# Rows of a mixture of experts sent to their expert's region batch by batch, the weights awaited by expert, one clearing of semaphores a stage, and three operations of the last stage put elsewhere

## The reference

```python
x = x + L0_attn(norm(x), W)                 # windowed attention
x = x + L0_xattn(norm(x), ctx, mask, ...)   # cross attention to 77 context rows, 8 heads
x = x + L0_ffn(norm(x), router_w, W1, W2)   # 8 experts, each row uses one:
    #   top1 = argmax(h @ router_w + router_b); y = gelu(h @ W1[top1] + b1) @ W2[top1] + b2
x = x + L1_attn(norm(x), ...)               # two-part mixing with a scan over batches (wkv)
x = x + L1_xattn(norm(x), ctx, ...)         # top-32 attention, FiLM, state-space convolution, network
x = x + L1_ffn(norm(x), ...)                # product with signs, scale, bias, clip to +-100
```

## Time and profile before

| | us |
|---|---|
| median of 3 runs (lowest, highest) | 1900.02 (1899.65, 1901.29) |
| the profiled execution, its own time | 1900.81 |
| the span that its trace covers | 1899.1 |
| PE busy, share of the span | 1632.9, 86% |
| DVE busy | 1312.9, 69% |
| ACT busy | 866.0, 46% |
| POOL busy | 655.4, 35% |

### The profile page before, as it was taken

The page is one execution under the profiler, slowest core; times in us unless marked ns, Lnnn a source line. Parts: engine busy times, 40 slices in busy tenths (PEclk is TensorE's granted clock), DMA queues, the critical chain, the costliest instruction groups (busy, mean ns, idle before and its releaser), DMA issues.

```text
span 1899.1 us, 26400 instructions
## 1 busy us (share of the span) xinstructions
PE 1632.9 (86%) x7946; PEld 1260.9 (66%) x7946; DVE 1312.9 (69%) x4214; ACT 866.0 (46%) x1714; POOL 655.4 (35%) x1016
## 2 busy tenths in 40 slices
PE   5899999993199999993677999999999999998775
PEld 3677777772066766772555777777778777776544
DVE  2467777764047777542567899898889899987642
ACT  1344444441022111113555666777766667754331
POOL 1122222212500000004444566556556555543221
PEclk9899999996599999997788999999999999999876
DMA  8000000004844343435000000000000000000000
GB/s 261 19 1 1 1 1 1 1 1 154 327 129 137 100 118 98 129 114 191 6 6 6 7 12 12 7 12 12 12 6 12 12 6 7 7 6 7 0 6 11
DMA packets 81060, 92.91 MB, mean 49 GB/s; under 512 B 19142, under 2 KB 69527, under 8 KB 80667
## 3 DMA queue, kind: packets, MB, share of 16 engines
q1 hardware_dynamic: 72235, 77.73, 12.8%
q0 software_dynamic: 3072, 8.39, 1.3%
q10 hardware_dynamic: 5616, 5.11, 0.8%
HBM read 70.76 MB, written 20.45 MB: 48 GB/s over the span
## 4 chain that ended last, share of the span: by engine, by line
PE 26%; DVE 20%; issue 3%; ACT 2%; POOL 2%; DMA 0%; POOLq 0%; DVEq 0%; ACTq 0%
PE E_pK L2218 5%; PE E_pK L2177 3%; PE E_pS L2279 3%; DVE E_wk L1748 3%; DVE E_ex L1680 2%; PE E_pY L2326 2%; PE E_pY L2165 2%; PE E_pY L2297 2%; DVE E_m L1741 2%; PE E_pU L2288 1%; DVE E_st L1613 1%; PE E_pY L2177 1%; PE E_pT L2159 1%; PE E_pY L2228 1%; PE E_pU L2316 1%
## 5 line engine op out<-in xcount | busy, mean ns | idle before, releaser
L1226 ACT ACTIVATE F_uT<-F_puT 128x512 f32<-128x512 f32 x78 | 42.8, 595 | 287.5 <-PE F_puT L1287 256.5
L1277 PE MATMUL F_pu<-C_W,F_hT 128*128 x312 | 145.3, 610 | 1.2 <-issue 1.2
L1498 POOL TENSOR_SCALAR E_var<-E_mv 128x2 f32<-128x2 f32 x80 | 42.1, 527 | 292.9 <-DVE E_mv L1617 291.8
L1297 PE MATMUL F_py<-C_W,F_uT 128*128 x624 | 141.3, 380 | 0.5 <-ACT F_uT L1226 0.5
L2316 PE MATMUL E_pU<-E_xT,E_W 128*128 128x256 f32 x512 | 121.5, 393 | 7.2 <-ACT E_hid L2075 4.9
L1297 PEld LDWEIGHTS F_py<-C_W,F_uT 128*128 128x128 f32 x624 | 115.9, 191 | 15.0 <-issue 1.2
L2228 PE MATMUL E_pY<-E_Wcv,E_hid 128*128 128x256 f32 x512 | 119.6, 389 | 4.0 <-issue 2.4
L2228 PEld LDWEIGHTS E_pY<-E_Wcv,E_hid 128*128 128x128 f32 x512 | 97.2, 195 | 28.9 <-issue 16.7
L2316 PEld LDWEIGHTS E_pU<-E_xT,E_W 128*128 128x128 f32 x512 | 101.1, 198 | 22.9 <-ACT E_hid L2075 5.7
L2326 PE MATMUL E_pY<-E_W,E_hid 128*128 128x256 f32 x512 | 115.6, 380 | 0.0
L2218 PE MATMUL E_pK<-E_cmix,E_Wck 128*128 128x256 f32 x512 | 115.3, 380 | 0.0
(11 more groups left out here) (408 smaller groups left out, 4295.4 us busy)
## 6 DMA issues: line engine op xcount, KB each, us to landing
F_b<-in_L_ffn_b SPq DMA_DIRECT2D x39, 512.0 KB, 4.3
C_W<-in_L_ffn_W SPq DMA_DIRECT2D x16, 1024.0 KB, 13.9
sorted_x<-zero SPq DMA_DIRECT2D x1, 4992.0 KB, 19.6
F_xs<-sorted_x SPq DMA_DIRECT2D x39, 128.0 KB, 2.3
F_b<-in_L_ffn_b SPq DMA_DIRECT2D x39, 128.0 KB, 3.1
sorted_y<-F_y ACTq DMA_DIRECT2D x39, 128.0 KB, 2.2
out<-E_tB SPq DMA_DIRECT2D x16, 256.0 KB, 2.1
X<-in_x SPq DMA_DIRECT2D x3, 1024.0 KB, 10.7
```

The source lines that it names most:

```text
L1277: last = nc.tensor.matmul(p_u[:, f, :], hT[:, i % 2, kb, :], W1[:, bass.ds(e, 1), kb, f * 512:(f + 1) * 512], start=kb == 0, stop=kb == KD ...
L1297: last = nc.tensor.matmul(p_y[:, 0:D], uT[:, f, :], W2[:, bass.ds(e, 1), f, :], start=f == 0, stop=f == FB - 1)
```

## The change

Router and sending. The first stage now also counts: `count(i)` on DVE keeps running sums of the one-hot rows, `ranks(i)` on PE makes two products of 16 columns that give each row its number within its expert, `number_rows(i)` on DVE picks it and adds 4,096 times the expert, and POOL sends the batch's two tiles by indirect DMA in the same stage. `sorted_x` has a region of 4,096 rows for each expert, so 32,768 KB are zeroed in eight DMAs. `place_rows` keeps only the counting of blocks, with a table `source` of the row at which each block begins. Each expert has at least one block, so block i is never of an expert above i; the loads of matrices have a semaphore an expert and are issued by ACT, expert 0 in placing, 1 to 4 after the third block of rows has landed, 5 to 7 after the first blocks. The semaphores of a stage are cleared together in the stages of attention and of experts (the joint stage keeps its six groups).

```diff
+            def count(i):                                   # DVE
+                dve.wait_ge(r["hot"], i + 1)
...
+                ve.tensor_tensor(seen[:, 2 * i + 1, :], seen[:, 2 * i, :], hot[:, 2 * i, :], ALU.add).then_inc(r["seen0"], 1)
+                dve.wait_ge(r["seen0"], i + 1)
+                ve.tensor_tensor(seen[:, 2 * i + 2, :], seen[:, 2 * i + 1, :], hot[:, 2 * i + 1, :],
+                                 ALU.add).then_inc(r["seen"], 1)
+            def number_rows(i):                             # DVE
+                dve.wait_ge(r["rkp"], i + 1)
+                for t in range(2):
+                    last = ve.tensor_tensor_reduce(picked[...], rank_place(i)[...], hot[...],
+                                                   1.0, 0.0, ALU.mult, ALU.add, rank[...])
+                last.then_inc(r["rk"], 1)
+                dve.wait_ge(r["rk"], i + 1)
+                ve.scalar_tensor_tensor(out=target[...], in0=atf[...], scalar=float(B * S),
+                                        in1=rank[...], op0=ALU.mult, op1=ALU.add).then_inc(r["target"], 1)
+            def ranks(i):                                   # PE
...
+                te.matmul(to, tri[:], hot[...], start=True, stop=False)
+                te.matmul(to, ones[:], seen[...], start=False, stop=True).then_inc(r["rkp"], 1)
             def turn_B(i):                                  # PE
                 pe.wait_ge(b["h"], i + 1)
                 past(pe, r["lg"], i - 3)
+                past(pe, r["rk"], i - 4)
+            LATER = {7: (0, 1), 8: (2, 3)}                  # POOL; then one batch a round
+            def scatter(i):
+                pool.wait_ge(r["target"], i + 1)
+                if i == 0:
+                    pool.wait_ge(ld["zeroed"], 16 * E)
+                for n in (2 * i, 2 * i + 1):
+                    nc.gpsimd.indirect_dma_start(...)
-                engine.dma_start(xs[:, i % XB, :], xs_dram[i * P:(i + 1) * P])
+            at = engine.value_load(source[0:1, i:i + 1], ...)
+                engine.dma_start(xs[:, i % XB, :], xs_dram[bass.ds(at, P)])
+            act.wait_ge(dma["xs2"], 16)                     # ACT, experts
+            for e in range(1, AHEAD):                       # AHEAD = 5
+                load_expert(act, args, W1, W2, loaded, e)
             gelu(0)
+                if i < E:                                   # PE, first(i)
+                    pe.wait_ge(loaded[i], 32)
-            pe.wait_ge(loaded, 32 * E)
```

```diff
+                if 0 <= i < LAST:                           # POOL, LAST = B - 3
+                    spectrum(i)
+                if i >= LAST:                               # DVE, end of its own spectrum(i)
+                    dve.wait_ge(e["tAB"], i + 1)
+                    ... the same four additions, on DVE
+            def bounded(p):                                 # DVE
                 dve.wait_ge(f["z"], p + 1)
                 chained(v.tensor_scalar(ob, ob, 100.0, -100.0, ALU.min, ALU.max))
@@ DVE, round n
                     add_mix(t + 1)
+                if 0 <= p < B:
+                    bounded(p)
@@ ACT, round n
-                if t + 1 < B:
-                    h_1(t + 1)
...
                     queries(c)
+                if t + 2 < B:
+                    h_1(t + 2)
```

216 lines of the change are left out of this document (133 added, 83 removed).

## The result

The changed kernel takes 1875.96 us in the median of 4 runs (1873.23 to 1880.01); the kernel before took 1900.65 beside it (1899.65 to 1904.17). The ratio is 0.987, with a 95% interval of 0.986 to 0.989: faster by 24.7 us, 1.3%, clear of the noise. The forecast was 1855, range 1842 to 1871. The direction holds; the gain is little more than half of what was forecast, and the time lies outside the range.

A forecast was written before the change was run, and what follows sets the result against it. PE bounds attention, only placing fills a 66.9 us gap, DVE and PE share the joint path. From span 1899.1, -46.0 + 6.0 + 2.0 - 0.5 - 6.4 = -44.9 gives 1854.2, adjusted to 1855; range 1842 to 1871.

The forecast's parts named there:

- the zeroing: First stage: zeroing 32,768 KB takes 129 us, done at 160, before the first send at 204.6, so hidden.
- The experts' +2.0: Experts' stage: FiLM and kernel constants share the DMA engines with the weights; 2.0 us lost, bounds 0 and 12.
- at 1.9 us each it is free 14.9 us later: Experts' start: ACT issues eight loads in 14.9 us, making the first GELU 6 us late; PE waits 1 to 2.
- the third rival: Experts: weights come late, loads at half rate beside the first blocks; 10 to 15 us, 1867; chance 0.11.
- The joint stage's -6.4: Joint stage: moving the clip and last addition, the first norm of mixing and the last three spectra wins 6.4 us.
- the early norm: Joint stage, first four rounds: `h_1` taken off ACT ahead of the exponentials wins 1.0, 1.0, 0.9 and 0.5 us.
- the steady rounds: Joint stage: moving `bounded` wins only 0.1 of 1.1 us a round, 1.2 us in 12 rounds.
- the last rounds: Joint stage's end, last three spectra on DVE: 2.5 and 0.3 us won, 1.0 lost.
- The gap's -46.0: From the last one-hot rows to the experts' first product: 20.9 us instead of 66.9; bounds 41 and 50.
- The tail, the placing and the first block: Parts of the gap: tail of the first stage 5.1 us, placing 6.7, first block 8.1.
- The first stage's +6.0: First stage: `count` costs 1.2 us, `turn_B` waiting for `rk` 4.8 over twelve rounds; together 6.0 lost.
- rival 1: First stage pays more: `rk` delays router rows and norms, counting comes to the front; 14 us, 1863; chance 0.14.

The follow-up runs named there:

- the second trace: The changed kernel run and traced once more, with nothing altered: 1876.04 us.
- number_first: Against the changed kernel, DVE in the first stage picks the numbers of a batch's rows ahead of the next batch's choice of experts: 1868.34 us.

## Why the forecast was wrong

The order of events was the forecast one. Sends ran from 204.7, `turn_B` waited for DVE, the zeroing hid, the clears and the last batch's counting took what they were given. Three terms failed, and one was right by accident.

**The experts' +2.0 (measured 13.4).** The step that failed is "at 1.9 us each it is free 14.9 us later". The 1.9 was read from the first eight issues of before, when nothing but the matrices was being loaded. The first three of them cost 0.4 to 0.6 us, the fourth 1.0, the fifth and seventh 4.7 and 5.5, and the eighth megabyte landed 27.9 us after the first issue. In the changed kernel the eight start from an empty queue again (expert 0 had landed at 474.80, they start at 477.77), but beside the biases and rows of the first blocks: the eighth megabyte lands 32.9 us after the first issue, and ACT is free not after 14.9 us but after 20.9. Its table load of 1.28 us stands behind the issues as well. So the GELU came 11.9 us late instead of 6. Expert 1 landed 3.2 us late instead of in time, the next three 6 to 7.5 us apart, the last three 9.5 to 11. From then on the rows shared the way with 14.7 MB that were never laid against them. This was the third rival, at 0.11, with its price of 10 to 15 us. What the experiments show of the 13.4 us is the part of ACT's issues, 3.5 to 5.7 us of the stage; that the rest belongs to rows that land late beside the matrices is read from the traces. The issue time of a DMA is an engine's time: the Trainium skill says that to issue from several engines saves only the time on the sequencer, "which is usually small relative to the DMA itself" (DMA: Bandwidth & Descriptors, Issuing engines are not separate DMA queues). Here single issues took up to 5.9 us, against 16.3 us to the landing of that load, and halving their number ahead of the GELU gave 7.2 us; the measurement decides.

**The joint stage's -6.4 (measured -0.2, or -5.8 in the second trace).** The edits did what was forecast in sum: the early norm 2.1 to 3.1 us instead of 3.4, the steady rounds a loss of 0.02 to 0.04 each instead of a gain of 0.1, the last rounds 2.6 to 3.2 instead of 1.8. What the sum lacked was the clock in the third round: PE's wait of 11.4 us was there before as well, with 13.7 us at half clock in and behind it; the three edits do not shorten that stretch, and with them it was 17.1 or 23.9 us long. None of the three edits undone alone brought 13.7 back, so which of them lengthens it is open. The clock stood in the trace of before, and I priced no term by it.

**The gap's -46.0 (measured -43.6).** The tail, the placing and the first block came as forecast within 1 us. Missing was GpSimd's drain, 2.8 us past its last dispatch; of these, moving the last two sends gave back 2.1. In the kernel before the drain is in the trace as well: GpSimd waits for the landings until 507.5, then drains for 2.67 us (507.65 to 510.32), and every engine's barrier waits for it. It lay in the 7.8 us between the last issue and 511.04, which the sum took as the time that the landings need.

**The first stage's +6.0 (measured +6.3).** The wait of `turn_B` cost 0.2 us a round, half of what I took. The larger half of the sum is clock: low stretches in the middle of the stage that before did not have, and that number_first removed together with the wait. The right number came from a wrong split, and rival 1, "the first stage pays more", was near for a reason that it did not name: in four of the thirteen traces with that wait the stage pays 9.

The range ended at 1871 because each rival was added alone to a sum that was otherwise right; here rival 3 at its full price and a lost term of the joint stage came together.

## What to carry to other kernels

Where a compute engine issues large loads ahead of its own work, take the time of its issues from a stretch with the same other loads beside them, and keep few of them in front of the first operation that others wait for (here four instead of eight, 7.2 us). A small new wait on the engine that carries the path is worth more than its length when the trace shows that engine's clock falling after idle time; look for the order that hides it (here: pick the numbers before the choice, 4 to 8 us of the stage for three moved lines), and put idle products into a single long wait whose clock loss can be read. Where software DMAs end a stage, look at the drain of the engine that issues them, not only at their landing.

## What the runs showed of the hardware

- GpSimd's drain at a stage's end lasted 2.8 us past its last indirect DMA, and 5.8 us where expert 0's two megabytes were loading beside it.
- A product of 512 float32 columns with 128 rows took 0.87 us at full clock (12 in 10.46 us) and stands in the trace as two instructions.
- The stretch at half clock that begins in one and the same wait of 11.4 us lasted 17.1 us in one trace and 23.9 in another of the same kernel, and 13.7 in all three traces of the old joint order. What decides between them is open.
- With a wait of 0.3 us more in each round of the first stage, every one of thirteen traces had two to four stretches of 3.4 us at half clock between 200 and 400 us; none of the five traces without it had any there.
- Eight loads of 1 MB issued in a row held the issuing engine for 14.9 us where nothing else was loaded, and for 20.9 us beside the biases and rows of the first blocks.
